# A two-layer graph network on one core: count matrix in blocks of 125 sources, and norm, router and dispatch in one phase

## The reference: what is computed

```python
# layer 0, graph block: six gated steps over the graph
for _ in range(6):
    h = jnp.maximum(node_feats @ W1.T + b1, 0.0) @ W2.T + b2
    msg = jax.ops.segment_sum(h[src], dst, num_segments=n_nodes)
    gx, gh = msg @ W_ih.T + b_ih, node_feats @ W_hh.T + b_hh
    ...                                    # gates r, z, n
    node_feats = (1.0 - z) * n + z * node_feats
# layer 1, feed-forward block: 8 experts, hidden size 682, two per node, on the normalised x
probs = softmax(xn @ router_w.T)
weights, picked = top_2(probs)             # weights divided by their sum
out[node] += sum over its 2 experts: weight * (silu(xn @ w1[e].T) * (xn @ w3[e].T)) @ w2[e].T
```

## Time and profile before

| | |
|---|---|
| median of 3 runs | 4265.12 us (4263.03 to 4272.1) |
| profiled execution | 4288.9 us, span 4287.0 us |
| mean granted TensorE clock | 0.952 of 2.4 GHz |
| TensorE matmuls busy | 3770.9 us, 88% |
| VectorE busy | 2588.5 us, 60% |
| ScalarE busy | 1499.6 us, 35% |
| GpSimd busy | 781.9 us, 18% |
| DMA | 302.47 MB, 71 GB/s over the span |

### The profile page before, as it was taken

How to read it: one execution, slowest core, us unless ns; L and a number is a source line. 1 busy time by engine, 2 the same in 40 slices (tenths; PEclk the granted TensorE clock), 3 DMA queues, 4 the chain that set the end, 5 groups by cost and what they waited for, 6 DMA issues and landing times. The chain is left out here.

```text
span 4287.0 us, 63922 instructions
## 1 busy us (share of the span) xinstructions
PE 3770.9 (88%) x19431; PEld 3115.3 (73%) x19432; DVE 2588.5 (60%) x4981; ACT 1499.6 (35%) x3667; POOL 781.9 (18%) x611
## 2 busy tenths in 40 slices
PE   2888878999999999999996799697999999339995
PEld 1444446989989899898995688455888888338884
DVE  7766485555565555655555555545777776436665
ACT  0123221121121211211111444345887773125552
POOL 0000000000000000000000200006888883041110
PEclk9999898999999999999998899898999999569998
DMA  3123212323323233232330211003333331421112
GB/s 110 24 60 72 64 45 86 90 68 87 88 71 87 75 87 87 71 88 75 87 87 13 73 31 31 28 25 77 91 90 89 88 88 36 166 72 36 36 37 106
DMA packets 318721, 302.47 MB, mean 71 GB/s; under 512 B 108504, under 2 KB 294045, under 8 KB 317807
## 3 DMA queue, kind: packets, MB, share of 16 engines
q1 hardware_dynamic: 258437, 226.34, 18.9%
q0 software_dynamic: 56288, 65.77, 5.8%
q10 hardware_dynamic: 3722, 6.88, 0.5%
HBM read 244.73 MB, written 53.75 MB: 70 GB/s over the span
## 5 line engine op out<-in xcount | busy, mean ns | idle before, releaser
L950 PE MATMUL bank<-a_wide,parts 128*128 128x448 f32 x4200 | 871.8, 367 | 0.0
L950 PEld LDWEIGHTS bank<-a_wide,parts 128*128 128x128 f32 x4200 | 786.6, 188 | 76.2 <-issue 10.7
L2083 POOL DMA_INDIRECT rows<-h_dram,src_t x400 | 523.0, 1308 | 123.2 <-issue 108.6
L2199 ACT ACTIVATE hot<-eq,ea 125x80 f32<-125x80 f32 x1600 | 413.3, 350 | 0.0
L910 POOL TENSOR_TENSOR nf_g<-nf,nf_g 128x896 fp32r<-128x896 f32 x42 | 94.5, 2250 | 1623.1 <-ACT nf_g L1110 1623.1
L1018 DVE CAST a_wide<-a_cols 128x2240 fp32r<-128x2240 bf16 x210 | 274.4, 1323 | 141.2 <-PE bank L950 141.2
L959 PE MATMUL bank<-nf_g,whh 128*128 128x448 f32 x1512 | 338.5, 368 | 0.0
L959 PE MATMUL bank<-msg,wc 128*128 128x448 f32 x1512 | 337.5, 367 | 0.0
L748 DVE TENSOR_SCALAR hot_at<-iota_at,edge_at,tile_at 125x1000 f16 x516 | 256.4, 545 | 130.8 <-PE bank L784 84.2
L2125 PEld LDWEIGHTS bank<-prod,hot 125*80 125x80 f32 x2400 | 295.3, 150 | 53.7 <-issue 0.7
L2125 PE MATMUL bank<-prod,hot 125*80 125x128 f32 x2400 | 328.4, 273 | 0.0
(11 more groups left out here) (376 smaller groups left out, 5763.0 us busy)
## 6 DMA issues: line engine op xcount, KB each, us to landing
a_cols<-a_dram SPq DMA_DIRECT2D x210, 560.0 KB, 4.2
a_dram<-a_cols SPq DMA_DIRECT2D x16, 1250.0 KB, 7.9
w<-in_w SPq DMA_DIRECT2D x4, 2728.0 KB
deg_bc<-deg_dram SPq DMA_DIRECT2D x42, 224.0 KB, 3.2
gate_bc<-gate_dram SPq DMA_DIRECT2D x42, 224.0 KB, 3.3
x_b<-x_slots SPq DMA_DIRECT2D x56, 132.0 KB
x_slots<-no_rows SPq DMA_DIRECT2D x1, 7168.0 KB
rows<-h_dram,src_t POOLq DMA_INDIRECT x400
```

Source lines behind the costliest of these rows:

```text
L950: ins = nc.tensor.matmul(p_msg[f][:, 0:GW], parts[:, m, c * HB + k, f * 128:(f + 1) * 128], a_wide[u % 2][:, k, :], start=(c == 0 and k == ...
L2083: nc.gpsimd.indirect_dma_start(out=rows[n % ITC][:, :], out_offset=None, in_=h_dram, in_offset=bass.IndirectOffsetOnAxis(ap=src_t[:, n:n + ...
L2199: ins = nc.scalar.activation(hot[:, q % 2, j, m, :], eq[:, q % 2, j, :], ACT.Copy, scale=ea4[:, q * UC + j, m:m + 1])
```

## The change

Two parts. In the first, the sources are cut into 25 blocks of 125 (`SPB`) in place of 128. `hot_lo` has 125 rows of marks and row 125 is all ones, so that row 125 of the count matrix is the number of edges per destination and source block. The degrees are summed from it after the loop, by a matmul over [125, 640], and the largest entry tells whether a count could pass 256. The degree matmuls, `nil`, `edge_sum` and the zeroing of `x_slots` are gone. ScalarE computes `edge_rel` = `edge_at` + `tile_at` for five tiles ahead. A tile has a first visit, a loop, and a last visit with `stop=True`, each with its own buffers (two, `SLOTS` = 2, two); it has at least three visits (`SPAN` = 6). "n0" now follows `adjacency`. In `gated_graph` the loads, casts and matmuls use partitions 0 to 124.

In the second, the statistics of the last norm are made at the end of `edge_convolution`, and `route_to_blocks` replaces "n3", "r1" and `dispatch`. The normalised rows and the two weights of each node go to `xn_dram` in node order. The slots are inverted on the chip: for each row tile and choice VectorE makes a one-hot row of the place in the block and two of the block number, one times the row number and one times the pair's index, and TensorE accumulates their product in one bank [128, 112]. From it come `x_idx` and `y_idx`. `expert_swiglu` gathers `x_b` on GpSimd by `x_idx`, and picks the weight by `choice`.

```diff
@@ adjacency, VectorE
-                    slot = hot_at[:, bass.ds(v & (SLOTS - 1), 1), :, :].rearrange("p o c w -> p (o c) w")
-                    dve.wait_ge(used, START + v - (SLOTS - 1))
                     for c in range(2):
-                        ins = nc.vector.tensor_scalar(slot[:, c, :], iota_at[:, :], edge_at[:, bass.ds(u + c, 1)],
-                                                      tile_at[:, bass.ds(t, 1)], ALU.subtract, ALU.is_equal)
+                        ins = nc.vector.tensor_scalar(slot[:, c, :], iota_at[:, :], edge_rel[:, j % RELS, bass.ds(u + c, 1)],
+                                                      None, ALU.is_equal)
...
+                        dve.wait_ge(rel_done, START + t + 1)
+                        dve.wait_ge(first_used, START + t - 1)
+                        marks(t, j, hot_first[:, j % 2, :, :], first).then_inc(first_done, 1)
                         fetch(dve, at, j + 1, t + 1)
+                        with dve.Fori(first + 2, past - 2, 2) as u:
+                            v, slot = mid_slot(dve, turns)
+                            dve.wait_ge(mid_used, START + v - (SLOTS - 1))
+                            marks(t, j, slot, u).then_inc(mid_done, 1)
+                            dve.reg_add(turns, turns, 1)
+                        dve.wait_ge(acc_mm, START + t - 1)
+                        marks(t, j, hot_last[:, j % 2, :, :], past - 2).then_inc(last_done, 1)
@@ adjacency, TensorE
+                        turn(to, hot_first[:, j % 2, :, :], first, True, False).then_inc(first_used, 1)
+                        fetch(pe, at, j + 1, t + 1)
+                        with pe.Fori(first + 2, past - 2, 2) as u:
+                            v, slot = mid_slot(pe, turns)
+                            pe.wait_ge(mid_done, START + v + 1)
+                            turn(to, slot, u, False, False).then_inc(mid_used, 1)
+                            pe.reg_add(turns, turns, 1)
+                        pe.wait_ge(last_done, START + t + 1)
+                        turn(to, hot_last[:, j % 2, :, :], past - 2, False, True).then_inc(acc_mm, 1)
@@ adjacency, SP, behind the last stores
+                counts = a_dram[SPB:SPB + 1, :, :]
+                sp.dma_start(by_cut[:, :], counts.rearrange("o k (c n) -> (o k c) n", c=CUTS)).then_inc(rows_in, 16)
+                sp.wait_ge(deg_done, START + 2)
+                sp.dma_start(deg_dram.rearrange("(c n) -> c n", c=CUTS), deg[:, :]).then_inc(deg_out, 16)
@@ gated_graph
-                            sp.dma_start(a_cols[u % 3][:, :, :], a_dram[:, c * HB:(c + 1) * HB, cols]).then_inc(a_in[u % 3], 16)
+                            sp.dma_start(a_cols[u % 3][0:SPB, :, :], a_dram[0:SPB, c * HB:(c + 1) * HB, cols]).then_inc(a_in[u % 3], 16)
@@ route_to_blocks, TensorE
+                def turn(t):
+                    pe.wait_ge(normed, START + t + 1)
+                    pe.wait_ge(copied, START + t - 1)
+                    for k in range(KD):
+                        ins = nc.tensor.transpose(p_x[t % 2][:, k * RT:(k + 1) * RT], xn[:, t % (NT - GT), k * 128:(k + 1) * 128], ident[0:RT, 0:RT])
+                    ins.then_inc(turned, 1)
+                def scores(t):
+                    pe.wait_ge(copied, START + t + 1)
+                    for k in range(KD):
+                        ins = nc.tensor.matmul(p_lg[0:RT, t * 8:t * 8 + 8], xt[:, t % 2, k, :], w1[:, k, :],
+                                               start=(k == 0), stop=(k == KD - 1))
+                    ins.then_inc(lg_mm, 1)
...
+                for i in range(NT * TOP):
+                    pe.wait_ge(marked, START + i + 1)
+                    nc.tensor.matmul(p_id[:, 0:2 * NBLK], hot_place[:, i % SETS, :], hot_block[:, i % SETS, :, :].rearrange("p a b -> p (a b)"),
+                                     start=(i == 0), stop=(i == NT * TOP - 1)).then_inc(used, 1)
@@ route_to_blocks, VectorE, in place of the 50 scatters
+                for t in range(NT):
+                    for c in range(TOP):
+                        i = t * TOP + c
+                        dve.wait_ge(used, START + i - SETS + 1)
+                        nc.vector.tensor_scalar(hot_place[:, i % SETS, :], place_b[:, :], place_of[:, c, t:t + 1], None, ALU.is_equal)
+                        nc.vector.tensor_scalar(hot_block[:, i % SETS, 0, :], block_b[:, :], block_of[:, c, t:t + 1], row_f[:, :],
+                                                ALU.is_equal, ALU.mult)
+                        nc.vector.tensor_scalar(hot_block[:, i % SETS, 1, :], block_b[:, :], block_of[:, c, t:t + 1], float(i + 1),
+                                                ALU.is_equal, ALU.mult).then_inc(marked, 1)
@@ expert_swiglu, GpSimd
+                def rows(n):
+                    pool.wait_ge(xt_mm, START + n - RING + 1)
+                    pool.wait_ge(weight_done, START + n - RING + 1)
+                    nc.gpsimd.indirect_dma_start(
+                        out=x_b[:, n % RING, :], out_offset=None, in_=xn_dram,
+                        in_offset=bass.IndirectOffsetOnAxis(ap=x_idx[:, n:n + 1], axis=0)).then_inc(x_in[n % RING], 16)
```

More of the change, by code:

```diff
@@ L52 @@
 TC = TT * DW
-PAD = 4
+PAD = 8
 NCP = NCH + PAD
-SLOTS = 4
+SPAN = 6
+RELS = 5
+CUTS = 5
+SLOTS = 2
 HB = 5
@@ L820, in _, with relative @@
             @block.scalar
             def _(act):
+                def relative(t, b):
+                    nc.scalar.activation(edge_rel[:, b, :], edge_at[:, :], ACT.Identity, bias=tile_at[:, bass.ds(t, 1)], scale=1.0)\
+                      .then_inc(rel_done, 1)
+                for t in range(RELS):
+                    relative(t, t)
                 with act.Fori(0, NM) as g:
```

576 lines of the change are left out of this document (327 added, 249 removed).

## The result

The changed kernel takes 4137.66 us (median of four runs, 4135.64 to 4138.31) against 4266.26 for the kernel before on the same chip: a ratio of 0.9696, 95% interval 0.9679 to 0.9713. The forecast was 4197 with a range of 4172 to 4236. The direction came out as written, and of the stages that the kernel decides only the count matrix missed by more than about 5 us; the gain is 61 us larger than the sum, nearly all of it in the loop of the count matrix.

What follows compares the result with a forecast made beforehand. TensorE was taken to bound graph, experts and count matrix, a dependency chain the dispatch. Terms 0.3 - 5.5 + 0 + 7 + 0 + 0.8 - 70.5 + 0 = -67.9 us, from the median 4265.12, gave 4197; range 4172 to 4236.

Steps and rivals of the forecast that it cites:

- the new tile of 3.93 us: Count matrix loop: a tile of three visits costs 3 x 1.17 + 0.42 us; all 80 tiles take 380 us.
- The bound below: Count matrix loop: the fetch is hidden behind queued work in most tiles, 80 x 0.3 = -24 us.
- I take 0: Count matrix loop: 38 new visits cost 44 us, less overhead per tile saves 45; priced at no change.
- Start and end of the count matrix: TensorE starts after 3.1 us, -5.5 us; new loads, maximum, copy and store behind the last store add +7.
- Rival A: Gated graph: the five-engine loads become the bound, 8.1 us a load, +250 us, about 4447; 7 in 100.
- Norm, router and dispatch: From the norm's start to the first expert block 87 us in place of 157.5, -70.5; clock expected to rise.
- What was priced at nothing: Expert blocks: GpSimd issues two DMAs per block in place of one, rows still come early; 0 us.
- The base: Whole kernel: the profiled execution lies 23.8 us above the median, so 4221.0 when profiled becomes 4197.
- The +0.8 us for the statistics: Edge convolution: 25 statistics add 12.5 us to VectorE, hidden behind TensorE but for the last tile.
- C: Rival: the fetch hides better in the loop, -24 us, dispatch at its lower bounds, -7: 4166; 10 in 100.
- B: Rival of smaller gain: two slots and third visit +20, dispatch rounds +13, half clock +3 us: 4233; 20 in 100.
- D: Rival: the new dispatch chain takes as long as the old scatters, 4265; 2 in 100.

Runs made afterwards that it cites:

- a_loop_last: The changed kernel with each tile's closing visit back in the loop and the closing matmul on `nil` behind it: 4242.34 us, 0.9869 of before.
- a_fetch_late: The changed kernel with TensorE's two register loads for the next tile issued behind the closing visit: count matrix 341.1 us, +0.7.
- a_one_load: The changed kernel with a tile's first and past packed in one word, one register load in place of two: 4139.61 us, 0.963 of before.
- b_one_load: The kernel before with first and past packed in one word, one register load in place of two: 4236.22 us, count matrix 369.9 us.
- a_twice125: The changed kernel with every load of `a_cols` in the gated graph issued a second time into a spare tile: gated graph 2193.8 us, +540.
- b_last_out: The kernel before with only each tile's closing visit in straight-line code behind the loop, at least three visits a tile: count matrix 421.3 us, +21.6.

## Why the forecast was wrong, by its steps

**The loop: 380 us forecast, 320 measured.** The failed step is the new tile of 3.93 us, and in it the way over the register loads: "busy 1.07 and waits 0.81 for its own instructions", 1.88 us, which measured 1.37. The steps in the changed kernel:

```
step                                    forecast   measured   on all
first visit to the loop's first           1.88       1.37      -41
loop's last to the closing visit          1.00       0.91       -7
closing visit to the next first visit     1.05       0.85      -16
loop visit to loop visit (56)             1.17       1.24       +4
sum                                                            -60
```

The first line is 41 of the 60 us. I took the 1.88 from one row at 239.30 and carried it over to all 80 tiles of the new loop. As a reading of the kernel before it was right: the 16 tiles without degree matmuls take 1.90 on average there. What didn't hold is that the new loop keeps it. The step is 1.68 on average with the closing visit in the loop (`a_loop_last`), and 1.37 with straight-line code ahead of it.

The cause that the forecast named, TensorE's own instructions and the register loads among them, was right. The loads were moved (`a_fetch_late`) and halved (`a_one_load`, `b_one_load`), and the time followed each time. Wrong was how much of them shows: that depends on how far TensorE's instructions have run ahead of its matmuls. The trace has a measure for it, the start of a tile's first load against the start of its first visit. It starts 0.56 us after it in the kernel before (median), 0.20 after it in `a_loop_last`, and 0.23 before it in the changed kernel; the median step falls alike, 1.87 (the 16 tiles without degree matmuls), 1.53 and 1.09. So the straight-line closing visit, with buffers of its own and without `nil`, gives 0.43 us of the lead. The other 0.36 are already there in `a_loop_last`, whose first visit has fixed buffers of its own in place of a slot to be worked out. No run takes those buffers away alone, so what they give is not shown.

The third line is the same thing seen at the other side: between the closing visit and the next first visit, with no loop and no `nil` between them, the step is 0.85. The bound below, "the fetch hidden behind queued work", -24 us, was therefore no bound. TensorE's own work is: by the shortest step, 296 visits x 0.85 = 252 us. Had that stood in the range, it would have held the result.

That the 38 new visits and the dropped overhead cancel ("I take 0") fell with it. Removing the degree matmuls alone gives 1.8 us, the closing visit in straight-line code alone loses 21.6. Together, with `nil` gone, cheaper marks and buffers of their own for the first and the closing visit, they are worth 60. What each part gives beside the others wasn't separated further, and a sum of separately priced parts could not have shown it.

**Start and end of the count matrix.** 3.1 forecast, 3.2 measured; a pass over 408 columns took 0.64 us against 0.6. From the end of the last visit to the next phase it is 16.6 us, 2 under the 18.8 (11.8 + 7) of the forecast.

**125 rows.** Rival A fell: no VectorE wait for `a_cols`. A load takes 5.0 us against the 5.2 I took, far from the rival's 8.1 and from the 7.2 at which it would have decided. Five loads of 5.0 us on five of sixteen engines give a DMA share of 0.22, and the trace has 0.25: the loads' packets are 0.23 of it, the other rows' 0.02. That is the rule of the Trainium skill cited in the forecast ("DMA: Bandwidth & Descriptors"), and `a_twice125` agrees: there the casts wait for the loads at a DMA share of only 0.35, where five of sixteen is 0.31.

**Norm, router and dispatch.** -70.5 against -70.8 to the first transpose (157.5 to 86.7). One term was right for a wrong reason. I expected the clock to rise, since TensorE would be busy without gaps. It is busy 20.00 of 20.00 us from 3580 to 3600 and the granted clock stays at 0.50, 1.2 GHz. But a tile costs 1.17 us there, not 1.27, so 25 tiles took 30.0 us where I had 29, and TensorE began 0.6 us sooner than forecast. That the logits came on time at the half clock is luck.

**What was priced at nothing.** The expert blocks took 5.2 us more: 1.7 is the first gather, counted above; 4.6 stands at the end, where the next phase begins 13.5 us after the last scatter's issue in place of 8.9; the blocks between them take 1.1 less. The first norm gained 5.0 us behind the count matrix. Neither was tried.

**The base.** I took the profiled execution's 23.8 us above the median off the sum, without asking where they stood. They stood in one stage, the edge convolution, and the subtraction was right: without that stage the differences of the profiles add up to 128.1 us, the timed medians lie 128.6 apart. The +0.8 us for the statistics in that stage can't be told from the scatter: within a set the changed kernel and its variants are from 1.6 us shorter to 2.8 longer in that stage.

**The rivals.** C had the right direction, "the fetch hides better", with a size of 24 for what was 60, and its own value, 4166, already lay below the range that was said to take in most of it. B and D fell.

## What to carry to other kernels

A loop whose steps are about as long as its control instructions is priced from averages over all its turns, and a step's price holds only with the same code ahead of it. Its bound below is the engine's own work, not a share of one wait. Read a register once where two values fit in one word. Leave one visit of a short inner loop outside it, if that doesn't add visits and closing work: alone it lost 21.6 us here, with the rest of the change it was worth 74. Each showed tens of microseconds only because 80 tiles pay it. Before a stage's difference is explained, look whether the kernel before shows the same spread on another chip, and whether the profile was taken among the timed runs.

## What was unexpected

- Loading one register from SBUF holds TensorE's queue for 0.30 us in 126 of 162 cases and for 0.6 to 0.95 us in 34, at the same places of the program in most turns. One load less in a tile, on TensorE and VectorE, gave 0.37 to 0.38 us a tile in both kernels.
- With a matmul of two columns on one row between straight-line visits the step is 0.27 us longer (1.12 in `b_last_out` against 0.85 in the changed kernel), though that matmul is shown busy for 0.17. The two kernels differ in more than it.
- TensorE, busy for 28.9 us without a gap (3576.06 to 3604.92) with transposes and products of 8 columns, was granted 0.50, 1.2 GHz, throughout; it had been idle for 6.7 us before.
- The edge convolution takes 711 to 712 us in the set whose kernel before takes 4266 us, and 737 to 744 in the three where it takes 4292 to 4299, with either kernel.
